# A third buffer for the exponentials, with new issue orders, in a four-layer kernel with four attentions

## The reference

```
x = ln(x + time_mix(x))        # layer 0: RWKV-like mix, causal convolution
x = ln(x + picked_linear(x))   # one of 8 matrices
x = ln(x + attention_1(x))     # 16 heads of 8 channels, not causal
x = ln(x + experts_1(x))       # 8 experts, top 2, and a shared one
x = ln(x + attention_2(x))     # 16 heads, rotary, causal
x = ln(x + block_2(x))         # grouped attention (4 key heads), causal; then 8 experts, top 2
x = ln(x + attention_3(x))     # 4 key heads, ALiBi, causal
x = ln(x + ternary_ffn(x))     # hidden 512
```

```
p = softmax(scale * q @ k.T + mask_or_bias)
out = p @ v
```

## Time and profile before

| | |
|---|---|
| runs | 1131.44, 1136.6 and 1137.35 us, median 1136.6 |
| profiled execution | 1137.08 us |
| its span, first to last instruction | 1135.2 us |
| mean granted clock of TensorE | 0.93 of full speed |
| first attention (chain 1) | about 85 to 316 us |
| first experts | about 317 to 450 us |
| second and third attention (chain 2) | about 454 to 797 us |
| second experts | about 797 to 900 us |
| last attention (chain 3) | about 915 to 1082 us |

### The profile page before, as it was taken

One profiled execution on the slowest core, in us unless ns is written; L12 is line 12 of the kernel. 1 busy time (PEld: TensorE's weight loads), 2 busy tenths in 40 slices (PEclk: granted clock), 3 DMA queues, 4 the chain that ended last, 5 costly groups with the idle time before them and its releaser, 6 DMA issues.

```text
span 1135.2 us, 25530 instructions
## 1 busy us (share of the span) xinstructions
PE 992.1 (87%) x8020; PEld 480.0 (42%) x8024; DVE 837.0 (74%) x2567; ACT 674.1 (59%) x1361; POOL 404.7 (36%) x675
## 2 busy tenths in 40 slices
PE   3469898988889998889999999999989798999986
PEld 1213232322256664334444444443556433444354
DVE  5998889799445556778889888884333678988576
ACT  2207878776654442557777777666555257777552
POOL 5623252223314532444323332335135345321121
PEclk8659999999899998899999999998999769999899
DMA  6123444431112332222212412211233321220001
GB/s 164 33 79 118 156 161 137 145 106 34 42 51 64 103 98 65 82 63 86 93 52 69 176 38 61 66 38 44 64 95 87 100 73 53 69 68 25 2 1 38
DMA packets 85628, 88.10 MB, mean 78 GB/s; under 512 B 13100, under 2 KB 72204, under 8 KB 85304
## 3 DMA queue, kind: packets, MB, share of 16 engines
q1 hardware_dynamic: 69149, 71.90, 20.1%
q0 software_dynamic: 4160, 8.53, 2.6%
q10 hardware_dynamic: 12187, 6.05, 1.9%
HBM read 45.41 MB, written 40.11 MB: 75 GB/s over the span
## 4 chain that ended last, share of the span: by engine, by line
PE 46%; issue 20%; DVE 13%; ACT 7%; POOL 7%; DVEq 3%; POOLq 3%; DMA 1%; ACTq 0%; SPq 0%
PE bank L2472 10%; PE bank L2458 6%; PE bank L2433 4%; PE bank L2442 4%; PE bank L2408 4%; ACT PT L1442 3%; PE bank L2718 3%; PE bank L2692 3%; DVE M L1866 2%; DVE masked_scores L1863 2%; PE bank L2696 2%; POOL slots_x L1247 2%; PE bank L2703 1%; POOL SHARED L1263 1%; PE bank L2493 1%
## 5 line engine op out<-in xcount | busy, mean ns | idle before, releaser
L1442 ACT ACTIVATE PT<-bank 128x512 f32<-128x512 f32 (+2 forms) x832 | 417.2, 545 | 190.5 <-PE bank L2458 150.2
L1866 DVE TENSOR_REDUCE M<-bank 128x1 f32<-128x512 f32 (+1 forms) x448 | 258.2, 625 | 37.3 <-PE bank L2433 34.1
L2433 PE MATMUL bank<-KS,QS 61*128 61x512 bf16 (+3 forms) x1024 | 257.0, 338 | 22.2 <-DVE M L1866 11.0
L2458 PE MATMUL bank<-QS,KS 64*128 64x512 bf16 (+3 forms) x1024 | 249.6, 327 | 16.3 <-ACT PT L1442 13.7
L1863 DVE CUSTOM_DVE_ANT_0 masked_scores<-bank,maskw 128x384 bf16<-128x384 f32 (+1 forms) x384 | 220.1, 620 | 25.4 <-PE bank L2433 22.6
L2472 PE MATMUL bank<-PT,VA 128*32 128x512 f32 (+3 forms) x2048 | 223.1, 514 | 1.1 <-ACT PT L1442 0.7
L2442 PE MATMUL bank<-half_ident,half_mask 64*128 64x64 bf16 (+1 forms) x1536 | 151.2, 211 | 16.3 <-ACT PT L1442 10.4
L2442 PEld LDWEIGHTS bank<-half_ident,half_mask 64*128 64x128 bf16 x1536 | 79.9, 95 | 146.0 <-ACT PT L1442 80.6
L2433 PEld LDWEIGHTS bank<-KS,QS 61*128 61x128 bf16 x1024 | 80.0, 97 | 112.2 <-DVE M L1866 43.4
L2458 PEld LDWEIGHTS bank<-QS,KS 64*128 64x128 bf16 x1024 | 80.7, 96 | 82.5 <-ACT PT L1442 70.2
L1131 POOL CAST MS<-M 128x16 bf16<-128x16 f32 x64 | 12.8, 200 | 268.9 <-DVE M L1866 268.8
(11 more groups left out here) (307 smaller groups left out, 1472.4 us busy)
## 6 DMA issues: line engine op xcount, KB each, us to landing
QS<-scr_q SPq DMA_DIRECT2D x128, 96.0 KB, 2.3
slots_x<-XSB SPq DMA_DIRECT2D x32, 256.0 KB, 2.7
scr_q<-PQ SPq DMA_DIRECT2D x16, 384.0 KB
KS<-scr_k SPq DMA_DIRECT2D x64, 96.0 KB, 2.2
XSB<-slots_x SPq DMA_DIRECT2D x92, 64.0 KB, 1.8
slots_y<-YSB ACTq DMA_DIRECT2D x20, 256.0 KB, 2.4
scr_q<-PQ SPq DMA_DIRECT2D x16, 256.0 KB
MW<-in_m_w SPq DMA_DIRECT2D x9, 392.0 KB
```

The costliest lines, as they stand in the source:

```text
L1442: a.activation(PT[kt % 2][:, js[0]:js[-1] + 1, q0:T], tiles(bank[st_bank(L, g, i)][:, 0:w * len(js)], len(js)), ACT.Exp, scale=LAYERS[L][" ...
L1866: v.tensor_reduce(M[g % 2][:, t * GH + js[0]:t * GH + js[-1] + 1], tiles(src[:, 0:kl * len(js)], len(js)), AX_X, ALU.max, negate=True).the ...
L2433: r = mm(to[:, n * kl:(n + 1) * kl], QS[rows_of(j, ROWS_SHIFT), q_slot(g, j), t * P:(t + 1) * P], KS[rows_of(j, ROWS_SHIFT), kv_slot(L, g, ...
L2458: r = mm(to[:, n * w:(n + 1) * w], KS[rows_of(j), kv_slot(L, g, j), kt * P:(kt + 1) * P], QS[rows_of(j), q_slot(g, j), T - w:T], start=not ...
```

## The change

`PT` gets a third buffer. The buffer of a key tile is no longer `kt % 2` but the running number of the key tile modulo 3, which runs on over units and attentions, for the exponentials and for the values. An exponential now waits for the values of the key tile three back. The three tables are new in all rows; their lengths and the number of passes are as they were. Of them one row stands here.

```diff
+PT_BUFS = 3
+
+
+def pt_no(L, b, g, kt):
+
+    return (((b + NB * L) * NG + g) * NT + kt) % PT_BUFS
...
 SCORE_ORDER = {
...
-        "- T TTT T T TT - - - - T TT TT TT - -"],
+        "T T TT T T TT TT TT TT TT - - - - - -"],
...
-        PT = [sb(f"PT{i}", [P, GH, T]) for i in range(2)]
+        PT = [sb(f"PT{i}", [P, GH, T]) for i in range(PT_BUFS)]
...
-                at_least(act, pv_done, U(L, b, g) * NT + kt - 1)
-                a.activation(PT[kt % 2][:, js[0]:js[-1] + 1, q0:T], tiles(bank[st_bank(L, g, i)][:, 0:w * len(js)], len(js)), ACT.Exp,
+                at_least(act, pv_done, U(L, b, g) * NT + kt + 1 - PT_BUFS)
+                a.activation(PT[pt_no(L, b, g, kt)][:, js[0]:js[-1] + 1, q0:T], tiles(bank[st_bank(L, g, i)][:, 0:w * len(js)], len(js)), ACT.Exp,
                              scale=LAYERS[L]["scale"]).then_inc(exp_done, 1)
...
-                    r = mm(bank[4][32 * j:32 * (j + 1), q0:T], VA[:, kt, v_slot(L, g, j), :], PT[kt % 2][:, j, q0:T],
+                    r = mm(bank[4][32 * j:32 * (j + 1), q0:T], VA[:, kt, v_slot(L, g, j), :], PT[pt_no(L, b, g, kt)][:, j, q0:T],
```

More of the change, by code:

```diff
@@ L193 @@
[L193 to L200 removed]
+    0: ["1111111120000121", "1111211111233010", "0111211201111111", "2111121110011110",
+        "1111111101111111", "0101111011220000", "1112232301101110", "1230011111121111",
+        "1211111201110111", "0111111011113000", "2220023301111111", "1111111111111000",
+        "2222000125000000", "0000022111111111", "1200000000000000", "0000000000000000"],
@@ new lines @@
+    1: ["012441100100", "101022010112", "212212221111", "122000001121",
+        "201121100111", "011110000100", "101011560111", "111111211211",
+        "201121100111", "011110000010", "001111560000", "000112222222",
+        "211121200110", "110110100100", "101011550001", "000112221222"],
+    2: ["211111200111", "111110000010", "001111560101", "101111212121",
+        "211011210110", "110110001011", "011233330111", "111111111111",
+        "101112210101", "010110120312", "230111110111", "111011111100",
+        "112220040202", "300001100101", "010000000000", "000000000000"],
@@ L201 @@
+    3: ["223223000000", "000007011112", "212212221111", "110000101112",
+        "112112110101", "010110001110", "111222120111", "011112121221",
+        "212122000101", "010110001011", "011111341111", "111211111112",
+        "111111120101", "010110011111", "120000000000", "000000000000"],
 }
 EXPS_AT = {
-    0: ["1111114010101010", "1111211111111111", "1112111111111111", "2222200101010101",
-        "0111260000011111", "1111211121112111", "2112101101101101", "1011111201101111",
-        "1111224010111111", "1111101010111112", "1112011121112111", "2111201101101110",
-        "1111311111111112", "1111201101101101", "1011611111110111", "1101111110111111"],
@@ L216 @@
-    3: ["003301201111", "111110101010", "101161111111", "111120111110",
-        "111123300000", "111111111111", "111101111121", "111122220010",
-        "011123300000", "110111111111", "111120111111", "111112330010",
-        "010131111111", "111110111111", "111140110111", "111101111111"],
+    0: ["1111202011111111", "1101111111111211", "1112101111112121", "2121200101010101",
+        "0111242000011112", "1111211121112111", "2112001101101111", "0111111101101111",
+        "1111222121201111", "0111101010101111", "1111511111112111", "1111200011211112",
+        "1112012222201011", "0101101101101101", "1011611101110111", "1111110111111111"],
@@ new lines @@
+    1: ["122220012111", "111110010010", "010131121211", "212120110111",
+        "111201212000", "111110101101", "101150111111", "111111121121",
+        "121210101200", "110110110111", "011141111111", "111121220111",
+        "011140011200", "111111111111", "111121111111", "111111110111"],
+    2: ["111140112000", "111110111111", "111111111111", "111122230101",
+        "010140111100", "110111111111", "111220111111", "111111120111",
+        "011151100201", "111110101101", "101150111111", "111111120101",
+        "010160111110", "110111111111", "111220111111", "111111111111"],
@@ L220 @@
+    3: ["010141201111", "011110101101", "101151111111", "111121111110",
+        "111122300010", "111111111111", "111120111110", "111112330010",
+        "011122201010", "110110111111", "111131111111", "111121120111",
+        "011121111110", "110111111111", "111241120111", "011101110111"],
 }
```

24 lines of the change are left out of this document (removed), and 46 rows, old and new, of the table SCORE_ORDER.

## The result

| | before | changed |
|---|---|---|
| median | 1136.6 us | 1126.59 us |
| runs | 1131.44 to 1137.35 shown before the forecast, 7 in this comparison | 7, 1123.09 to 1130.71 |
| profiled execution | 1137.08 us | 1123.09 us, the shortest of its seven |
| mean granted clock | 0.930 | 0.936 |

The ratio is 0.9927 with an interval of [0.9909, 0.9945]: 8.3 us faster, between 6.3 and 10.3. The two medians by themselves are 10.0 us apart. The forecast was 1132.0, its range 1117 to 1144. The two profiled executions are 14.0 us apart, more than the medians, so not all of what their traces differ by belongs to the change.

A forecast was written before the change was run, and what follows sets the result against it. PE was taken to bound the attention stretches, with 57.8 us idle in 741. Terms -1.9 - 2.2 - 0.9 - 2.2 + 2.2 = -5.0 from 1137.1 gave 1132.1, stated as 1132.0 us; range 1117 to 1144, the forecast's own 1127 to 1137.

The forecast's parts named there:

- the prediction's own last sign: A total outside 1127 to 1137 us, or a first attention's end still taking 13.8 us, makes the forecast wrong.
- Waits for values in mid-stage: PE's idle behind exponentials held up by full buffers, seven pieces behind six places, can go: -1.9 us, between 0 and -1.9.
- End of the first attention: Last unit: exponentials run on and three groups of values follow together; gain 1.7 to 3.2 us, taken as -2.2.
- should take 11 to 12 us: Sign: the first attention's end, from the pass at 301.88 to the last values, with one run of three groups last.
- The other two ends: Ends of the third and last attention: PE's idle of 0.58 and 0.36 us goes; -0.9 us, between 0 and twice that.
- Groups of values side by side: Separate runs of value groups fall from 239 to 227, at 0.27 us each; ten counted here, taken as -2.2 us.
- Bunches of passes: Close triples of transposed passes rise from 130 to 142, so PE waits more for emptied banks: +2.2 us, 0 to +4.4.
- PE's busy time in the attentions should hardly change: Sign: PE's busy time in the three attention stretches, 683.2 of 741 us before, should hardly change.
- neighbours on the same half: Neighbouring passes on the same half of the array's rows, which can't overlap, go from 299 to 304: no term.
- the whole order gets tighter: Rival, chance 0.20: exponentials run further ahead, a third of PE's 24.1 + 20.0 us idle goes too; 1117 us.
- runs of values starve ACT: Rival, chance 0.20: runs of two or more value groups go from 17 to 27, leaving ACT without scores; 1145 us.
- Nothing moves: Rival, chance 0.12: PE is the bound and does the same work, waits only shift between pieces; 1136.6 us.

The follow-up runs named there:

- the new row: Three buffers and the old tables with only the row of the first attention's last unit changed, against the kernel before: 1213.91 us beside 1219.18, ratio 0.9967.

## Why the prediction was right, and where not

The time lies inside the range and has the forecast's sign. The forecast's own range of 1127 to 1137 is missed by 0.4 us by the median of 1126.6, and by the prediction's own last sign that makes the forecast wrong; by the ratio (1136.6 - 8.3 = 1128.3) it is just met. The sum of -5.0 should have been about -8. That it came that near is in part luck: one term of 1.9 was worth nothing, and what replaced it was the clock and shorter pieces on PE, which the sum didn't have. By its steps:

- **Waits for values in mid-stage, -1.9: failed.** ACT's waits fell from 33.2 us to none that the list shows, as forecast (below 10), and yet the buffer alone gave nothing that can be measured (0.9995), and PE's idle behind exponentials fell by 0.5 us only. I had taken the seven pieces of PE's idle as owed to the full buffers, but the three that are shown stayed as they were. At 234.22, for one, ACT had waited 1.6 us for scores instead, and PE for ACT. My lower end, 0, was the right value.
- **End of the first attention, -2.2: right in its mechanism, mis-sized by the clock.** Three groups last, exponentials running on at 0.54 us each, as the forecast had it. The part that I had costed got 3.1 us shorter, inside my 1.7 to 3.2 and at the end that I had worked out for the full clock; "should take 11 to 12 us" was 10.75. The step that failed is "since PE stays as lightly loaded as before", by which I held the clock's level fixed and took the slow end. It went from 0.75 to 1.00 there, and from 0.89 to 1.00 in the 15 us ahead, which the sum didn't have at all and which gave another 1.8 us. Of the -4.9 at least 3.4 are clock, and the order's own part is at most 1.5.
- **The other two ends, -0.9: about right, as far as can be told.** At equal clock the end of the last attention is some 0.7 us shorter, with 0.6 of scatter left, and that of the third attention not at all. With the clock's scatter of 1.5 to 2.3 us in these stretches no median could show it.
- **Groups of values side by side, -2.2: mis-priced.** A change of layout and back costs 0.12 to 0.13 us and not 0.27, so twelve fewer are worth 12 x 0.13 = 1.6 at most, in part in the stage ends that were counted already. In the interior of chain 2 nothing was merged: by the records of PE the values of 104 groups stand in 98 separate runs before and in 99 after. The idle time of the weight load before a group isn't the price of a change. Changes of the array's rows or columns stand at other places too: by PE's records (rows up to 64 or 128, columns up to 32 or 128) the new order has 43 fewer of 818, six, 21 and 16 in the three chains. If all cost what the measured kind does, they come as half that many pairs at 0.12 to 2.6 us, near the term's size but by another count.
- **Bunches of passes, +2.2: little came.** PE's idle behind exponentials is 24.4 us in 73 places. That is 0.8 us above the 23.6 in 64 with the buffer alone, which has the old order.
- **The term that was missing.** I wrote that PE's busy time in the attentions should hardly change, and it fell: the interiors of chains 2 and 3 became 4.1 and 1.4 us shorter, all of it busy time. Some 1.5 us of it is the spell at the lower clock that the new order doesn't have. For the other 2.6 and 1.4 the sentence that failed is that 57.8 us of idle time is "all that a better order could win in them, unless pieces on PE become shorter", with neighbours on the same half "nothing worth a term". A piece's time on PE depends on what stands next to it.

What makes those pieces shorter is only partly settled. Two causes can be priced. The layout changes: 15 fewer in the interior of chain 2 and 8 fewer in the last attention's, so 7.5 and 4 pairs at 0.13, 1.0 of the 2.6 us and 0.5 of the 1.4. And neighbouring passes on different halves of the array's rows overlap. By the records of the first attention before, the matmuls of two passes that follow one another directly start a median 0.077 us apart on different halves (0.003 where the pass ahead of them is neither a score nor a maxima pass, 0.222 where halves already alternate) and 0.227 on the same half. With the values kept in the order and other pieces left out, chain 2 has in the new order 133 pairs on the same half, where the old one had 152, worth some 19 x 0.15 = 2.9 us, so together with the layout already more than the 2.6. But in the last attention the same count rises from 58 to 72, which asks for a loss of 2 us where 1.4 were gained. So the overlap is only argued as a cause, and the last attention speaks against it. An order with the same counts but different neighbours would have told, and wasn't tried. What makes the matmuls of the two interiors take less time, beyond the clock and the layout, stays open.

**The rivals.** That the whole order gets tighter (1117) had the right sign, and its half of the gain in the interiors is there. But its mechanism, a third less idle time behind exponentials and maxima, isn't: that went from 44.1 to 40.5 us, and the part behind exponentials didn't fall (24.1 to 24.4). That runs of values starve ACT (1145) didn't come: in mid-stage they cost nothing that PE shows, 24.4 us is far from the 30 at which it would have been right. Nothing moves (1136.6) is excluded by the interval, but holds for the buffer without its tables.

## What to carry to other kernels

Before a buffer is credited with an engine's waits, ask what that engine waits for next: 33.2 us of waits for space turned into 33 us of waits for data, because the engine wasn't the bound. The buffer still was what one row of the new order needed. Where an order of work is changed, compare the length of stretches between landmarks that the order leaves alone, since interiors agreed to 0.5 us here where single executions scatter by 9, and don't take the busy time of TensorE as fixed. Compare them at equal granted clock, and don't round it away: 0.99 and 1.00 over 266 us were 1.5 us apart. In a lightly loaded end of a stage, read the granted clock first: the group of values that took 1.58 us there takes 0.96 at the upper level.

## What was not expected of the hardware

- At the end of the first attention, in the part where 24 added matmuls without use ran, the stretch was 1.8 us shorter (11.66 instead of 13.50), at a granted clock of 1.00 instead of 0.75, and a group of values took 0.96 us instead of 1.58. This is from one trace.
- In one trace of the new row the clock fell some 2 us behind a halt and stayed at its lower level for 17 us (0.50 from 303.8 to 320.9), although PE had the denser order.
- One short spell at the lower clock (0.91 over 18.5 us) costs 1.5 us in a stretch where TensorE is the bound, and it is counted as busy time (19.20 instead of 17.68 us).
- A change of the array from 64-row to 32-column layout and back costs 0.12 to 0.13 us where TensorE is the bound.
- The same 1072 matmuls count as 89.1 or 87.1 us of busy time by their order, at a clock of 1.00 in both.
- Under one order, interiors of 92 and 266 us came within 0.5 us of the kernel before's from one execution to the next, while starts and ends of stages move by 1.5 to 9 us. The time of a whole execution follows its mean granted clock: over 33 runs of the kernel before, 1131 to 1140 us, the two have a correlation of -0.92.
